# One transformer layer on one core: output projection on 32 columns, late value projections moved, more half groups on VectorE, output bias ahead of the GpSimd reduction

## What is computed

```python
Q, K, V = X @ Wq + bq, X @ Wk + bk, X @ Wv + bv      # X: (1, 2048, 256), 16 heads of 16
scores = einsum('bhqd,bhkd->bhqk', q, k) / sqrt(16)
out = einsum('bhqk,bhkd->bhqd', softmax(scores), v)
out = out.transpose(0, 3, 2, 1).reshape(b, s, 256)   # head dimension outermost
x = layernorm(X + out @ Wo + bo)
y = silu((x @ w_gate) * s_gate) * ((x @ w_up) * s_up)
x = layernorm(x + (y @ w_down) * s_down)
```

## Time and profile before

| | us |
|---|---|
| median of three runs | 600.29 |
| lowest, highest | 600.27, 601.55 |
| the profiled execution | 600.33 |
| its span, first to last instruction | 598.6 |
| start until the first exponential | 44.3 |
| attention (exponentials) | 44.3 to 494.6 |
| feed-forward part and end | 494.6 to 598.6 |

### The profile page before, as it was taken

One profiled execution on the slowest core, in us unless ns is written; L12 is line 12 of the kernel. 1 busy time (PEld: TensorE's weight loads), 2 busy tenths in 40 slices (PEclk: granted clock), 3 DMA queues, 4 the chain that ended last, 5 costly groups with the idle time before them and its releaser, 6 DMA issues.

```text
span 598.6 us, 10544 instructions
## 1 busy us (share of the span) xinstructions
PE 588.2 (98%) x3952; PEld 249.7 (42%) x3952; DVE 442.4 (74%) x812; ACT 506.6 (85%) x614; POOL 54.4 (9%) x51
## 2 busy tenths in 40 slices
PE   8999999999999999999999999999999999999995
PEld 7884222222222223223232322222323227988974
DVE  6673766989888767687676668888767696776876
ACT  4539999999999999999999999999999995253352
POOL 6606000000000000000000000003000001102021
PEclk9999999999999999999999999999999999999998
DMA  9466938112303020111211010112010000101102
GB/s 207 72 105 85 122 62 105 26 29 35 85 11 70 8 34 8 31 16 25 61 17 27 11 29 11 30 34 44 8 33 7 7 4 9 39 1 35 36 2 71
DMA packets 36185, 24.71 MB, mean 41 GB/s; under 512 B 24930, under 2 KB 30946, under 8 KB 35538
## 3 DMA queue, kind: packets, MB, share of 16 engines
q1 hardware_dynamic: 34740, 23.29, 23.1%
q10 hardware_dynamic: 1392, 0.72, 0.5%
HBM read 6.56 MB, written 4.33 MB: 18 GB/s over the span
## 4 chain that ended last, share of the span: by engine, by line
PE 96%; DVE 2%; ACT 1%; issue 0%; DMA 0%; SPq 0%; POOL 0%; POOLq 0%; ACTq 0%
PE ps L1254 42%; PE ps L1226 29%; PE ps L1363 10%; PE ps L1096 6%; PE ps L1340 4%; PE ps L1276 3%; PE ps L1067 1%; DVE attn_q L820 1%; PE ps L1294 1%; PE ps L1082 1%; ACT probs L654 0%; DMA out<-out_tmp 0%; SPq L511 0%; DVE xt_lo L722 0%; PE ps L1128 0%
## 5 line engine op out<-in xcount | busy, mean ns | idle before, releaser
L654 ACT ACTIVATE probs<-ps 128x1024 f32<-128x1024 f32 (+1 forms) x512 | 444.1, 1098 | 14.8 <-PE ps L1226 14.4
L1254 PE MATMUL ps<-probs,v_all 128*17 128x512 f32 x1916 | 269.0, 598 | 1.2 <-DVE attn_q L820 0.5
L1226 PE MATMUL ps<-q_slot,k_stack 51*128 51x512 f32 x1024 | 198.0, 458 | 0.0
L1226 PEld LDWEIGHTS ps<-q_slot,k_stack 51*128 51x128 f32 x1024 | 85.0, 184 | 220.1 <-ACT probs L654 206.1
L884 DVE TENSOR_SCALAR bits<-ps 128x512 int32<-128x512 f32 x66 | 45.5, 689 | 50.2 <-PE ps L1226 41.3
L1254 PE MATMUL ps<-poly,v_all 128*17 128x512 f32 x132 | 68.2, 599 | 0.0
L673 ACT ACTIVATE sg<-ps,sgate_c 128x512 f32<-128x512 f32 x32 | 22.0, 689 | 49.5 <-PE ps L1363 49.5
L1254 PEld LDWEIGHTS ps<-probs,v_all 128*17 128x17 f32 x1916 | 33.5, 95 | 61.2 <-issue 50.6
L908 DVE SCALAR_TENSOR_TENSOR poly<-poly,bits 128x512 f32<-128x512 f32 x66 | 47.2, 715 | 7.2 <-DVE poly L904 0.5
L904 DVE SCALAR_TENSOR_TENSOR poly<-poly,mant 128x512 f32<-128x512 f32 x66 | 45.7, 692 | 2.3
L895 DVE SCALAR_TENSOR_TENSOR poly<-mant 128x512 f32<-128x512 f32 x66 | 45.2, 684 | 0.0
(11 more groups left out here) (99 smaller groups left out, 452.9 us busy)
## 6 DMA issues: line engine op xcount, KB each, us to landing
q_slot<-qy SPq DMA_DIRECT2D x64, 64.0 KB
k_stack<-k_part SPq DMA_DIRECT2D x12, 256.0 KB
at_dram<-attn_q SPq DMA_DIRECT2D x64, 34.0 KB
at<-at_dram SPq DMA_DIRECT2D x8, 272.0 KB, 3.0
q_slot<-qy SPq DMA_DIRECT2D x64, 32.0 KB
x_tok<-in_L_attn_X SPq DMA_DIRECT2D x14, 128.0 KB, 5.9
k_stack<-k_part SPq DMA_DIRECT2D x12, 128.0 KB
out<-out_tmp SPq DMA_DIRECT2D x12, 128.0 KB, 2.2
```

Of the source, the lines that this page charges most:

```text
L654: nc.scalar.activation(probs[:, slot_of(g), first:2, :].rearrange("p a b -> p (a b)"), ps[:, 2 * ring + first:2 * ring + 2, :].rearrange(" ...
L1226: last = nc.tensor.matmul(ps[:, 2 * ring + half, :], k_stack[s % QUADS][base:base + ROWS, p, kt * P:(kt + 1) * P], q_slot[slot][base:base ...
L1254: last = nc.tensor.matmul(ps[32 * hh:32 * hh + VW, ACC, :], v_all[:, tiles[hh], NQ * (s % QUADS) + hh, :], prob, start=(kt == 0), stop=(kt ...
```

## The change

Six edits in one:

1. `project_out` of the first three blocks uses four matmuls of 32 weight columns instead of one of 128, each to its own 32 partitions of the bank. The last block's call stays.
2. The late value projections stand behind the second and the fourth score pair, instead of the first and the fourth.
3. `probs` gets a seventh slot, used by g == 3 alone, over memory that pair 7 does not read. The wait for `v_psum` moves from g == 3 to g == 4.
4. `poly_tiles` gives five tiles in steps 0 and 1 as well.
5. Six of the eight additions of `bo` stand on POOL ahead of the reduction, two behind it.
6. DVE's wait for all eight stands ahead of the first `ln1_add`, no longer ahead of the first exponential.

```diff
-        probs = place("probs", [P, HALVES, 2, CW], f32, at)
+        probs = place("probs", [P, HALVES + 1, 2, CW], f32, at)
...
-            return [6, 10, 13] if s == 0 else [2, 6, 10, 13] if s == 1 else [2, 5, 8, 11, 14] if s in (2, 3, 4) else [2, 6, 10, 13]
+            return [2, 5, 8, 11, 14] if s <= QUADS else [2, 6, 10, 13]
...
-            return (0, 2, 4, 1, 3, 5)[g % HALVES]
+            return HALVES if g == HALVES // 2 else (0, 2, 4, 1, 3, 5)[g % HALVES]
...
+            def add_bo(first, last):
+
+                for p in range(first, last):
+                    nc.gpsimd.tensor_tensor(x_tok[:, 2 * p:2 * p + 2, :], x_tok[:, 2 * p:2 * p + 2, :],
+                                            bo_b[:].unsqueeze(1).to_broadcast([P, 2, HID]), ALU.add
+                                            ).then_inc(bo_added, 1)
+
+            BO_FIRST = 6
+            pool.wait_ge(bo_loaded, 16)
+            pool.wait_ge(xt_ready, 2 * CH)
+            add_bo(0, BO_FIRST)
+
             pool.wait_ge(norms_ready, 3)
             nc.gpsimd.partition_all_reduce(norm_all[:], norm_qk[:], P, MAX_ACROSS).then_inc(norms_reduced, 1)
...
+            add_bo(BO_FIRST, TT // 2)
...
-                if g == 3:
+                if g == 4:
                     act.wait_ge(v_psum, TT // 2)
...
+                if c == 0 and b == 0:
+                    dve.wait_ge(bo_added, TT // 2)
                 dve.wait_ge(wo_psum, 2 * c + b + 1)
...
-            dve.wait_ge(bo_added, TT // 2)
...
+                dst = ps[:, out_bank(c, j // 2), half * HID:(half + 1) * HID]
                 for ko in range(KO):
...
+                    if c < LAST:
+                        for d in range(CH):
+                            last = nc.tensor.matmul(dst[UW * d:UW * (d + 1), :], at32[:, ko, CH * j + d, :],
+                                                    wo[:, ko, :], start=(ko == 0), stop=(ko == KO - 1))
...
                 scores(2 * u)
-                if u == 0:
-                    project_v(V_LATE)
                 scores(2 * u + 1)
-                if u == 1:
-                    project_v(V_LATE + 1)
+                if u < 2:
+                    project_v(V_LATE + u)
```

More of the change, by code:

```diff
@@ L1274, in project_out @@
                 half = j % 2
+                dst = ps[:, out_bank(c, j // 2), half * HID:(half + 1) * HID]
                 for ko in range(KO):
-                    last = nc.tensor.matmul(ps[:, out_bank(c, j // 2), half * HID:(half + 1) * HID],
-                                            at32[:, ko, CH * j:CH * (j + 1), :].rearrange("p d u -> p (d u)"),
-                                            wo[:, ko, :], start=(ko == 0), stop=(ko == KO - 1))
+                    if c < LAST:
+                        for d in range(CH):
+                            last = nc.tensor.matmul(dst[UW * d:UW * (d + 1), :], at32[:, ko, CH * j + d, :],
+                                                    wo[:, ko, :], start=(ko == 0), stop=(ko == KO - 1))
+                    else:
+                        last = nc.tensor.matmul(dst, at32[:, ko, CH * j:CH * (j + 1), :].rearrange("p d u -> p (d u)"),
+                                                wo[:, ko, :], start=(ko == 0), stop=(ko == KO - 1))
                 if half:
```

## The result

The changed kernel takes 601.76 us in the median of 12 runs (600.99 to 603.89). The kernel before, run beside it, takes 600.26 (599.52 to 601.55). The ratio is 1.0027, with a 95% interval of 1.0018 to 1.0036 (the ratios given here are those on record; they can differ by up to 0.0005 from the quotient of the medians). So it is slower, by about a quarter of a percent. Its runs are spread over 2.9 us, those of before over 2.0. The execution that was profiled is the fastest of the twelve: 600.99, span 599.2.

A forecast was written before the change was run, and what follows sets the result against it. ACT's exponentials were taken to pace attention, PE between output projection calls. From 600.3 us, less 1.3 (half groups), 0.5 (late projections), 2.4 (output projection), plus 4.6 (late scores) and 2.3 (clock): 603.0, range 599.8 to 606.

The forecast's parts named there:

- The price of the change of code: On POOL ahead of the reduction: change taken as 7.4 us, bounds 0 to 8.3, first scores 4.6 us later.
- the nearest row: The 7.39 us POOL idles behind the reduction, read as the change back and used as the price, 7.4.
- PE's start behind the written bound: Ahead of the first scores: PE was estimated to need 0.15 us to see a semaphore.
- the 6 to 8 that were to show it: Sign in the trace: POOL idle 6 to 8 us between the sixth addition and the reduction.
- The clock: At the first scores: PE idle 4.7 us, then the 1.2 GHz level, costing 2.3 us, bounds 0 and 2.7.
- The output projection: Twelve calls on 32 columns, each saving 0.2 us: 2.4 us, bounds 0.8 and 2.5.
- the 0.85 to 0.88 that were to show it: Sign in the trace: an output projection call takes 0.85 to 0.88 us rather than 1.06.
- The late projections: Around the second and fourth exponentials: less ACT idle time, worth 0.5 us, between 0 and 0.6.
- The half groups: Two more in step 0, one in step 1, 0.44 us each: 1.3 us, bounds 0.9 to 1.3.
- the likeliest case: At the reduction: price 7.4 us and the clock falls; 603.0 us, chance 0.60.
- case C: At the reduction: price nearer 6 us, PE idle 3.3 us, the clock stays; 599.3 us, chance 0.17.
- B: At the reduction: nothing has to be loaded, the configuration change is free; 596.1 us, chance 0.12.

The follow-up runs named there:

- the bias edit alone: The kernel before with six additions ahead of the reduction and DVE's wait for them moved to its first use, nothing else: 605.01 us, ratio 1.0076.

## Why the prediction was right, and where it was not

**Direction and place: right.** The loss is where the prediction put it, ahead of the reduction, and it eats what the other edits bring. The time lies within the range, 1.2 us below the value named. How much slower it is hangs on the clock: with PE kept busy the same edits take 599.94, ratio 0.9992, which is about equal.

**The price of the change of code: too high.** The step was to take the nearest row, 7.4 us, for a change in the other direction. The time from the configuration instruction to the next one is what the traces show; that POOL changes its code in it is a reading. The change towards the reduction took 5.88 in the changed kernel, and 5.45, 5.67, 5.79 and 5.81 in four others. The way back took 6.9 to 7.7. So the price was 1.5 us too high. PE's start behind the written bound was estimated at 0.15 us and took 0.37. Together the first scores came 3.25 us later and not 4.6, and the idle 5.88 lies just under the 6 to 8 that were to show it. The Trainium skill (GPSIMD Engine Reference, section Instruction dispatch) had 5.95 for it. Here the page was nearer than the row; it names no direction, and the row was of the other one. That the change is hidden where POOL waits anyway is confirmed by the kernel with three additions ahead: it starts on time.

**The clock: right in kind, mis-sized.** PE was idle for 3.2 us and not 4.7, and the fall then came in most runs, though not in all. It cost 0.8 to 1.8 us in the median, and 1.5 in the one trace that shows it behind this gap (the bias edit alone), against 2.3 foreseen. In the profiled execution it was zero, and there the prediction was wrong by its own sign: the scores behind the gap kept their spacing. Whoever reads that one trace would miss a term of the sum.

**The output projection: right.** 2.4 us foreseen, 2.4 measured alone, 0.20 a call in the trace. But the sign was put in the wrong place. From the call's start to the scores it is 0.98 us, not the 0.85 to 0.88 that were to show it. Of the 0.20, 0.12 lie between product and call, where the change of shape dropped out, and 0.08 behind the call's start, for which no trace shows the cause.

**The late projections: right.** 0.5 foreseen, 0.46 in the trace.

**The half groups: a term was missed.** Step 1 gave its 0.44 (27.63 - 27.20 = 0.43). In step 0 the two more half groups were to give 0.9 and gave 0.7, and 0.3 went at the end of the kernel. And the two additions behind the reduction ran beside the first of them and took 0.6 back. The prediction counted only that DVE no longer waits, and gave the additions no cost beside DVE. With six ahead the miss was small. It was hidden behind the first error: the fewer additions ahead, the more stand beside DVE.

**The sum, remade.** 600.3 - 2.4 (output projection) - 0.5 (late projections) - 1.1 (half groups) + 0.3 (end) + 3.25 (first scores) + 0.6 (additions beside DVE) = 600.45 without the clock. Two times in which the clock did not fall stand on either side of it: 600.99, the profiled execution, and 599.94, the median with PE kept busy. So the terms are good to some 0.5 us. With 0.8 to 1.8 for the clock the sum is 601.3 to 602.3, and 601.76 was measured. That the prediction came within 1.2 us is partly luck: first scores put 1.35 us too late and a clock term put 0.5 to 1.5 too high were offset in part by about 1.1 us that it missed (0.6 of contention, 0.5 with the half groups).

**Chances.** The time of 603.0 was the likeliest case; what came is between it and case C, whose price of about 6 us was the true one, though its condition that the clock stays was met in few of the twelve runs. B, that nothing is loaded, is refuted by five traces.

## What to carry to other kernels

A gap on GpSimd in front of an instruction of another kind is not free room: look for a configuration instruction in it, since work moved into the gap pushes the change of code out behind itself. Work on GpSimd that reads and writes SBUF can also take time from VectorE's SBUF-to-SBUF instructions beside it (0.43 us became 1.4 here), so give it a place where VectorE waits, not only one where GpSimd does. And an engine that is idle for some microseconds in some executions only costs a clock term that one profile may not show: compare the mean granted clock of all runs.

## What the runs showed of the hardware

An addition on GpSimd (128x512, float32) slows some instructions of VectorE beside it and not others. `bits<-ps`, which reads PSUM, stayed at 0.68 to 0.69 us. The ones from SBUF to SBUF went from 0.43 to 1.4 to 1.5, and those with two SBUF operands from 0.68 to 1.6 to 1.8. The additions themselves grew from 1.25 to 1.42 each (11.37 / 8). The Trainium skill says in GPSIMD Engine Reference, section Specifications, that the SBUF interfaces are shared with VectorE, and names just these: instructions in a two-port mode, or with two SBUF inputs. By the durations the traces agree: the instructions from PSUM kept theirs, and those with two SBUF inputs did not. Which mode the 0.43 us instructions run in no trace shows. The prediction gave this no term.

From GpSimd's configuration instruction to the next one it took 5.5 to 5.9 us towards the partition reduction (five traces) and 6.9 to 7.7 back (eight traces). The first was hidden where GpSimd had to wait for the norms anyway.

Whether the clock falls after an idle stretch of TensorE of about 3 us is not settled by the kernel: with 3.2 us it stayed in the profiled run and fell, by their mean clock, in at least eight of the eleven others. What decides it in one execution stays open.
